# Replicated Q and K rows written and read by dimension, then head; the causal mask of the score maxima added by VectorE

## What is computed

```python
x = x + cross_attention(layernorm(x), ctx)            # 8 sequences of 512 x 256, context 64 x 256, 16 heads of 64
z = layernorm(x)
# dense part, for each sequence, H = 16 heads, hd = 16
q = (z @ wq).reshape(b, s, H, hd)
k = (z @ wk).reshape(b, s, H, hd)
v = (z @ wv).reshape(b, s, H, hd)
scores = jnp.einsum('bqhd,bkhd->bhqk', q, k) / np.sqrt(hd)
scores = jnp.where(causal, scores, finfo.min)
attn = jax.nn.softmax(scores, axis=-1)
o = jnp.einsum('bhqk,bkhd->bqhd', attn, v).reshape(b, s, d)
h = z + rmsnorm(o @ wo, attn_norm_w)
dense = h + rmsnorm(silu(h @ w1) * (h @ w3) @ w2, ff_norm_w)
# sparse part: router over 8 experts, two of them for each token, their outputs weighted, then rmsnorm
x = x + dense + sparse
```

## Time and profile before

| | |
|---|---|
| median of 3 runs | 1511.2 us (1509.92 to 1518.62) |
| the profiled execution's own time | 1514.02 us |
| its span in the trace | 1512.2 us |
| granted TensorE clock, mean | 0.962 |
| PE busy | 1376.5 us (91%) |
| DVE busy | 811.6 us (54%) |
| ACT busy | 575.4 us (38%) |
| POOL busy | 601.4 us (40%) |
| chain that ended last: PE, DVE, DMA | 66%, 9%, 7% |

### The profile page before, as it was taken

The page is one execution under the profiler, slowest core; times in us unless marked ns, Lnnn a source line. Parts: engine busy times, 40 slices in busy tenths (PEclk is TensorE's granted clock), DMA queues, the critical chain, the costliest instruction groups (busy, mean ns, idle before and its releaser), DMA issues.

```text
span 1512.2 us, 22383 instructions
## 1 busy us (share of the span) xinstructions
PE 1376.5 (91%) x7229; PEld 891.4 (59%) x7230; DVE 811.6 (54%) x1652; ACT 575.4 (38%) x1214; POOL 601.4 (40%) x1051
## 2 busy tenths in 40 slices
PE   6886898999899989998999899989998789999995
PEld 6543556656665666566656665666566246666673
DVE  2625655754485358436753675366546623333348
ACT  2231553055306521641255036404540444344346
POOL 4312343253325332633254235423532435555544
PEclk8998899999999999999999999999999799999997
DMA  6054205200600060006001500240031424332245
GB/s 209 1 145 138 67 1 130 53 16 1 157 26 16 1 164 19 16 10 170 18 1 39 144 16 1 78 104 16 1 105 50 152 86 129 127 100 87 86 177 197
DMA packets 77529, 115.39 MB, mean 76 GB/s; under 512 B 24072, under 2 KB 65440, under 8 KB 74880
## 3 DMA queue, kind: packets, MB, share of 16 engines
q1 hardware_dynamic: 67120, 79.68, 18.7%
q10 hardware_dynamic: 3840, 16.78, 3.9%
q0 software_dynamic: 6480, 17.77, 3.3%
HBM read 70.22 MB, written 43.59 MB: 75 GB/s over the span
## 4 chain that ended last, share of the span: by engine, by line
PE 66%; DVE 9%; DMA 7%; POOL 5%; ACT 5%; issue 3%; SPq 3%; ACTq 0%; POOLq 0%; DVEq 0%
PE ps L1069 8%; PE ps L1033 8%; PE ps L907 7%; PE ps L888 6%; DVE nm L1519 5%; PE ps L993 5%; PE ps L955 4%; PE ps L1086 4%; PE ps L980 4%; DMA room<-parts_d 3%; PE ps L1043 3%; DMA parts_d<-room 3%; PE ps L921 2%; PE ps L1013 2%; SPq L531 2%
## 5 line engine op out<-in xcount | busy, mean ns | idle before, releaser
L1519 DVE TENSOR_REDUCE nm<-ps 128x2 f32<-128x256 f32 (+3 forms) x256 | 202.4, 819 | 103.3 <-PE ps L956 100.9
L1211 ACT ACTIVATE room<-ps 128x512 f32<-128x512 f32 x320 | 179.7, 598 | 157.0 <-PE ps L980 156.8
L1033 PE MATMUL ps<-hT,w 128*128 128x512 f32 x768 | 212.7, 421 | 0.0
L692 POOL TENSOR_SCALAR_AFFINE_SELECT room<-room 128x256 f32<-128x256 f32 (+1 forms) x320 | 121.5, 391 | 138.3 <-ACT room L1211 133.6
L955 PE MATMUL ps<-room 96*128 96x128 bf16 (+3 forms) x512 | 129.6, 315 | 44.2 <-DMA room<-parts_d 26.5
L1033 PEld LDWEIGHTS ps<-hT,w 128*128 128x128 f32 x768 | 144.7, 196 | 33.1 <-DVE hT L1547 2.0
L1235 ACT ACTIVATE room<-ps 128x512 f32<-128x512 f32 x64 | 37.2, 593 | 294.2 <-PE ps L1033 294.2
L1043 PE MATMUL ps<-w,room 128*128 128x256 f32 x512 | 137.6, 399 | 7.5 <-DVE room L1568 7.5
L1069 PE MATMUL ps<-room 128*128 x284 | 135.4, 599 | 2.4 <-ACT room L1263 2.4
L907 PE MATMUL ps<-room 128*128 128x256 f32 x512 | 123.1, 384 | 2.7 <-ACT room L1172 1.8
L888 PE MATMUL ps<-room,xnT 128*128 128x512 f32 x256 | 122.0, 601 | 0.0
(11 more groups left out here) (234 smaller groups left out, 2372.3 us busy)
## 6 DMA issues: line engine op xcount, KB each, us to landing
room<-parts_d SPq DMA_DIRECT2D x48, 256.0 KB, 5.3
room<-parts_d ACTq DMA_DIRECT2D x48, 256.0 KB, 5.7
room<-xs_d SPq DMA_DIRECT2D x71, 129.0 KB, 2.1
parts_d<-room SPq DMA_DIRECT2D x64, 128.0 KB
room<-pair_d SPq DMA_DIRECT2D x8, 1024.0 KB, 8.3
room<-in_L_ffn_ew SPq DMA_DIRECT2D x24, 256.0 KB, 5.5
xin<-in_x SPq DMA_DIRECT2D x8, 512.0 KB, 8.1
parts_d<-xnT SPq DMA_DIRECT2D x32, 128.0 KB
```

The source lines that it names most:

```text
L692: done(g.affine_select(out=w, in_=w, compare_op=ALU.is_ge, fill=0.0, base=0, pattern=[[0, 2]] * (blocks - 1) + [[1, P]], channel_multiplie ...
L1033: last = mm(bank(up_banks(b, m)[i]), w[:, x, k, m * P:(m + 1) * P], hT[:, y, k, :], start=((x, y, k) == terms[0]), stop=((x, y, k) == term ...
L1211: done(fn(prob[:, u * 512:(u + 1) * 512], bank(6 + n % 2), ACT.Exp), "b_exp")
L1519: done(v.tensor_reduce(nm[:, t, 2 * hp:2 * hp + 2], pair_ps, AX.X, ALU.max, negate=True), "a_max")
```

## The change

Three things change.

1. The columns of wq and wk are reordered, once, from head then dimension to dimension then head. The weights are loaded into yb (as w_heads), and VectorE copies them into wq and wk ahead of the first "qk" step. TensorE's first "qk" waits for both copies. A projected part then has its rows by dimension, then head, so each store into parts_d is 128 rows of 1 KB with one stride on the DRAM side ("(d h) n"), where it was 8 heads of 16 dimensions.
2. Each set of six loads becomes three, of three, two and one places (REPLICAS). K's take parts 0 to 2, then 0 and 1, then 0; Q's take one part to three, two and one places by a repeat (stride 0) of the source. The places are no longer interleaved: place j has partitions 16 j to 16 j + 15. The six products of parts are the same ones.
3. Step "max": the mask matmul goes. VectorE adds mask_qk to the last 128 columns of both heads in the bank, linked, and then takes the maximum.

```diff
@@ -40,8 +40,7 @@
 PBUF = 4
 EW_EARLY = 6
 
-Q_PART = (0, 0, 1, 1, 0, 2)
-K_PART = (0, 1, 0, 1, 2, 0)
+REPLICAS = ((0, 3), (3, 2), (5, 1))
 
 UNITS = 10
 CHUNKS = 3
@@ -54,8 +53,8 @@
     sc_ps=4, sc_add=4, sc_sub=4, sc_exp=4, sc_rec=4, sc_nrm=4,
     pT_ps=8, pT_sb=8, pv_ps=4, xb=1, x1=4, mv2=4, rstd2=4, xn2=4, xT2=2, xn2T=2,
     qk_ps=4, part1=4, rest1=4, part2=4, part3=4, v_ps=4, v_sb=4, lg=4,
-    q_out=96, k_out=96, rep_q=96, rep_k=96, z=1,
-    gmax=1, gexp=1, mask=1, rank_ps=1, slot=1, xk=1, scat=128, dve_step=42, pool_a=4, pool_n=1,
+    q_out=96, k_out=96, rep_q=48, rep_k=48, z=1,
+    gmax=1, gexp=1, mask=1, rank_ps=1, slot=1, xk=1, scat=128, dve_step=74, pool_a=4, pool_n=1,
     a_ps=32, a_max=32, m_part=2, mT_ps=2, mT_sb=2, m_row0=48, m_row1=48,
     b_ps=G * UNITS, b_exp=G * UNITS, b_cut=G * UNITS, va_ps=G * CHUNKS, av_sb=4, avT_ps=4, o_rec=4, o_nrm=4,
     oT_ps=2, oT_sb=2, wo_ps=2, wo_sq=2, wo_ri=1, wo_n=2, hb=1, h=2, yb=1, hT_ps=2, hT_sb=2, hT_lo=2,
@@ -311,6 +310,7 @@
         xk_id = part(11264, T * XW).rearrange("p (t w) -> p t w", t=T)
         yb = sb("yb", [P, T, D])
         hb = sb("hb", [P, T, D])
+        w_heads = yb[:, :, :].rearrange("p t d -> p (t d)").rearrange("p (i k n) -> p i k n", i=2, k=KD)
         xnT = sb("xnT", [P, KD, S])
         xn2T = sb("xn2T", [P, KD, S])
         o_tok = sb("o_tok", [P, T, D])
@@ -469,8 +469,8 @@
             load_x(0)
 
             def load_late_weights():
-                for dst, src in ((wq, "L0_ffn_wq"), (wk, "L0_ffn_wk")):
-                    sp.dma_start(dst[:, :, :], A[src].rearrange("(k p) n -> p k n", p=P)).then_inc(p0["w_late"], 16)
+                for dst, src in ((w_heads[:, 0, :, :], "L0_ffn_wq"), (w_heads[:, 1, :, :], "L0_ffn_wk")):
+                    sp.dma_start(dst, A[src].rearrange("(k p) n -> p k n", p=P)).then_inc(p0["w_late"], 16)
                 sp.dma_start(wv[:, :, 0:D], A["L0_ffn_wv"].rearrange("(k p) n -> p k n", p=P)).then_inc(p0["w_late"], 16)
                 sp.dma_start(wv[:, :, D:D + E], A["L0_ffn_router_w"].rearrange("(k p) n -> p k n", p=P)).then_inc(p0["w_late"], 16)
                 for dst, src in ((wo, "L0_ffn_wo"), (w2, "L0_ffn_w2")):
@@ -521,14 +521,13 @@
                     for a in range(4):
                         for i, name in enumerate(("part1", "part2", "part3")):
                             need(sp, b, name, a + 1)
-                            done(sp.dma_start(parts_d[i, a // 2, :, :, a % 2, :].rearrange("d h n -> h d n"), parts[i][:, a, :]), ("q_out", "k_out")[a // 2], 16)
+                            done(sp.dma_start(parts_d[i, a // 2, :, :, a % 2, :].rearrange("d h n -> (d h) n"), parts[i][:, a, :]), ("q_out", "k_out")[a // 2], 16)
                     if c is not None:
                         need(sp, c, "b_ps", per["b_ps"])
                         sp.sem_inc(freed, 1)
                     need(sp, b, "k_out", per["k_out"])
-                    for j in range(NREP):
-                        src = parts_d[K_PART[j], 1, :, :, :, :].rearrange("d h a n -> d (h a n)")
-                        done(sp.dma_start(k_rep[j:KREP:NREP, :, :].rearrange("d h n -> d (h n)"), src), "rep_k", 16)
+                    for i, (j, n) in enumerate(REPLICAS):
+                        done(sp.dma_start(k_rep[j * HD:(j + n) * HD, :, :].rearrange("p h n -> p (h n)"), parts_d[0:n, 1, :, :, :, :].rearrange("i d h a n -> i d (h a n)")), "rep_k", 16)
                     if not (isinstance(b, int) and b == B - 1):
                         if c is not None:
                             load_kv(b + 1)
@@ -915,6 +914,7 @@
                         if a == 0:
                             if c is None:
                                 pe.wait_ge(p0["w_late"], 16 * 9)
+                                pe.wait_ge(p0["w_turned"], 2)
                             need(pe, b, "xn2T", 2)
                         w = (wq, wk)[a // 2]
                         for k in range(KD):
@@ -952,8 +952,7 @@
                         for i in range(2):
                             h = 2 * hp + i
                             o = nmax % 2 * 2 + i
-                            mm(bank(o, n), q_rep[0:KREP, rep_at(h), t * P:n], k_rep[0:KREP, rep_at(h), 0:n], start=True, stop=False)
-                            last = mm(bank(o, P, t * P), ident_b[:, :], mask_qk[:, :], start=False, stop=True)
+                            last = mm(bank(o, n), q_rep[0:KREP, rep_at(h), t * P:n], k_rep[0:KREP, rep_at(h), 0:n], start=True, stop=True)
                         done(last, "a_ps")
                     elif kind == "shift":
                         i = step[1]
@@ -1197,9 +1196,8 @@
                         if c is not None:
                             need(act, c, "b_ps", per["b_ps"])
                         need(act, b, "q_out", per["q_out"])
-                        for j in range(NREP):
-                            src = parts_d[Q_PART[j], 0, :, :, :, :].rearrange("d h a n -> d (h a n)")
-                            done(act.dma_start(q_rep[j:KREP:NREP, :, :].rearrange("d h n -> d (h n)"), src), "rep_q", 16)
+                        for i, (j, n) in enumerate(REPLICAS):
+                            done(act.dma_start(q_rep[j * HD:(j + n) * HD, :, :].rearrange("p h n -> p (h n)"), parts_d[i, 0, :, :, :, :].rearrange("d h a n -> d (h a n)").unsqueeze(0).to_broadcast([n, HD, H * S])), "rep_q", 16)
                         need(act, b, "gmax", 1)
                         done(fn(g_b, g_a, ACT.Exp), "gexp")
                     elif kind == "sc":
@@ -1451,6 +1449,9 @@
                         if a == 0 and c is None:
 
                             dve.wait_ge(p0["w_late"], 16 * 9)
+                            for i, w in enumerate((wq, wk)):
+                                v.tensor_copy(w[:, :, :].rearrange("p k (a d h) -> p (k a) d h", a=KD, d=HD),
+                                              w_heads[:, i, :, :].rearrange("p k (a h d) -> p (k a) d h", a=KD, d=HD)).then_inc(p0["w_turned"], 1)
                             for w in (aw_bc, fw_bc, mw_bc):
                                 v.tensor_scalar(w[:, :], w[:, :], float(D) ** 0.5, None, ALU.mult).then_inc(p0["norms"], 1)
                             dve.wait_ge(p0["norms"], 3)
@@ -1516,6 +1517,7 @@
                         need(dve, b, "a_ps", nmax + 1)
                         o = nmax % 2 * 1024
                         pair_ps = ps[:, o:o + 1024].rearrange("p (i n) -> p i n", i=2)[:, :, 0:(t + 1) * P]
+                        link(v.tensor_tensor(pair_ps[:, :, t * P:], pair_ps[:, :, t * P:], mask_qk[:, :].unsqueeze(1).to_broadcast([P, 2, P]), ALU.add))
                         done(v.tensor_reduce(nm[:, t, 2 * hp:2 * hp + 2], pair_ps, AX.X, ALU.max, negate=True), "a_max")
                     elif kind == "shift_parts":
 
```

More of the change, by code:

```diff
@@ L213, in xattn_ffn @@
         kv_out = [sem(f"p0_kv_out{i}") for i in range(4)]
-        p0 = {n: sem("p0_" + n) for n in ("w_first", "bias_ps", "w_early", "w_mid", "w_late", "w_up", "kv0_ps", "norms", "split_hi", "split", "ident", "const", "iota", "tr_ps", "tr_sb", "kv_ps", "kv_sb", "bk")}
+        p0 = {n: sem("p0_" + n) for n in ("w_first", "bias_ps", "w_early", "w_mid", "w_late", "w_turned", "w_up", "kv0_ps", "norms", "split_hi", "split", "ident", "const", "iota", "tr_ps", "tr_sb", "kv_ps", "kv_sb", "bk")}
         moe = {n: sem("moe_" + n) for n in ("table_step", "table", "ids_off", "ids", "ew_in", "zero", "gate", "xT_ps", "xT", "up_ps", "th", "u", "g", "gT_ps", "gT", "dn_ps", "eo")}
```

## The result

The changed kernel takes **1844.6 us** (median of 4 runs, 1842.0 to 1850.5), beside 1512.4 for the kernel before: a ratio of 1.219, 95% interval [1.215, 1.224]. The forecast was 1769, range 1730 to 1900. Both of its terms have the sign and the order that were forecast; the one for the loads was too small.

A forecast was written before the change was run, and what follows sets the result against it. It took the loads of Q and K ahead of each first max matmul as the bound: 1514.0 profiled + 192 for loads + 66 for the mask = 1772, less 2.8 to the median, 1769 us; range 1730 to 1900.

The forecast's parts named there:

- the one for the loads: Q's and K's loads ahead of the first max matmul end 24.0 us later a batch, 192 us over eight batches.
- What bounds the kernel: Ahead of the max stage the loads end last, by some 4 us a batch, so any delay is paid in full.
- The number of engines: A transfer uses the smaller outermost count: 3 engines for three places, 2 for two, 16 for the last load and stores.
- The rate of an engine: Each of the few engines moves 26.4 GB/s, so 1,081,344 bytes on the busiest take 41.0 us; 18.9 GB/s kept in range.
- The first walk: The first max there, without a network ahead, also comes 24 to 25 us later because of the loads.
- The effects taken as nothing: Earlier stores (perhaps 4 us), three fewer issues a queue (0.6 us each) and later loads behind K's: no effect on time.
- SP's queue behind K's loads: The kt_d and vt_d loads and x land after 435 instead of around 411, at no cost.
- The mask: In the max stage, VectorE's 32 additions at 0.46 us add 8.3 us a batch, 66 in all.
- The weights: Two copies of 512 elements on VectorE, once, before the first scalings: 0 to 1 us, taken as 0.
- The signs to look for: Profile after: load windows at DMA share 0.12 to 0.2, near 1 during stores, additions 0.42 to 0.5 us, stage about 51.
- All engines: Rival: the loads spread over all engines, first max 3.5 us earlier, VectorE's 8.3 remain: about 1550 us, chance 0.10.

The follow-up runs named there:

- the dimension-outermost run: Changed kernel with the mask on TensorE and three loads a set with the 16 dimensions as outermost count, places 3, 2 and 1 apart: 1554.6 us, ratio 1.024.

## Why the prediction was right, and by how much a term was off

- **What bounds the kernel.** Right. The loads ended last ahead of the max stage by 4 us, and all of what was added to them was paid: +268 us of distance, +269 us of time (the run with the mask on TensorE).
- **The number of engines.** Right, 3 and 2. The windows show 0.19 and 0.13, and the dimension-outermost run, with as many loads of the same size on 16 engines (its places differ too), takes the wait from 52 us to 23.
- **The rate of an engine.** Right for most of the wait, 26.4 to 27.0 GB/s for the 26.4 assumed. The step that failed is "so I take 26.4: 41.0 us" for the whole of the busiest engine's work. From the first load of Q to the first max it took 52 us, and 33.5 more than before instead of 24.0: 76 us over eight batches, as much as the whole miss (1845 - 1769). I had reasoned that few engines don't press the memory, and looked at the source side alone. The runs show that the third loads account for 1.4 to 2.6 us a batch of it and the small rows for about 1 at most. With both out of the way some 6 us are left: rows that took 0.9 to 1.5 us at the start and around 494 to 500 instead of 0.62 make 3.5 of them, and what slows these rows is not known. That the time came within the range is the doing of the range, which allowed for 18.9 GB/s an engine, and not of the point forecast.
- **The first walk.** Right that it loses as much as the others: 33.3 us.
- **The effects taken as nothing.** Stores: nothing to be seen in this kernel, where the loads wait for engines anyway; alone, with the weights, they are a gain, as the 1492.8 us show. Issues: nothing. SP's queue behind K's loads: its vt_d issue stood for 42.65 us, under the cover of the loads themselves.
- **The mask.** Right: 7.7 us a batch for 8.3, 0.46 us a step, VectorE's waits for TensorE inside the stage 41.9 - 39.4 = 2.5 us where "below 3" was forecast, the stage at 51.9 for "about 51".
- **The weights.** Right: nothing, the last store of the first walk was issued by 92.5 where it was 95.1.
- **The signs to look for.** The share of "near 1 while the stores run" did not come: 0.71 at most in the third batch. A store lands in 1.8 us and the parts come one after another, so the engines aren't full.
- **The rival that I priced wrongly.** "All engines" was put at 1550. The run that made it real, six loads to the same blocks, took 1657.5. It left out that a block of 16 consecutive partitions takes only 131 GB/s; it carried over what the places 6 apart had shown. For 48 rows that the chip spreads by itself there is no run. The nearest are this one, 107 us above 1550, and the dimension-outermost one, whose 1554.6 with the mask's 65 is about 1620 (an estimate), 70 above.

## What to carry to other kernels

Before merging DMAs, write down the outermost count of both sides: in all these runs the transfer ran on as many engines as the smaller has (2, 3, 8, and 16 for 16 or more), so a leading repeat or part index of 3 turned sixteen engines into three. Then look at where the engines' rows land at one time: rows 6 partitions apart came in nearly twice as fast as rows in a block of 16. An engine with much idle time in the span may have none in the stage where work is added; read its waits there.

## What the runs showed that I had not expected

- The destination partitions set a load's rate at the same number of engines: 122 to 131 GB/s for a block of 16, 217 to 262 for 16 places 6 apart. In the kernel before, this edit alone costs 85 us.
- Behind the long loads an issue itself can take long: SP stood on the two vt_d issues for 42.65 us, and the next batch's input was issued only after that. In this kernel it is covered.
- Stores with the outermost count 128 on both sides land in 1.8 us. In the kernel before, with 8 on one side, the last one took 6.76.
